# Query projection of the 32-head attentions by a seven-product block scheme, with single-buffered weights

## The reference, cut to what matters

```
q = rope(x @ Wq)      # 32 heads of 128: 512 -> 4096
k = rope(ctx @ Wk)    # 8 key heads of 128, each shared by 4 query heads
v = ctx @ Wv
p = softmax(q k^T / sqrt(128) + mask)      # per head and block, 128 x 128
x = layernorm(x + concat_heads(p v) @ Wo)  # 4096 -> 512
```

## Time and profile before

| | |
|---|---|
| median of 3 runs | 2799.91 us (2798.87 to 2800.82) |
| profiled execution, its own time | 2801.92 us |
| span of the profiled execution | 2800.6 us |
| mean granted TensorE clock | 0.987 of full speed |
| PE busy | 2658.8 us, 95% of the span |
| DVE, ACT, POOL busy | 59%, 30%, 16% |
| chain that ended last | PE 87%, DVE 7%, ACT 3% |

### The profile page before, as it was taken

How to read it: one execution, slowest core, us unless ns; L and a number is a source line. 1 busy time by engine, 2 the same in 40 slices (tenths; PEclk the granted TensorE clock), 3 DMA queues, 4 the chain that set the end, 5 groups by cost and what they waited for, 6 DMA issues and landing times.

```text
span 2800.6 us, 40463 instructions
## 1 busy us (share of the span) xinstructions
PE 2658.8 (95%) x15768; PEld 1764.9 (63%) x15768; DVE 1652.9 (59%) x3113; ACT 852.1 (30%) x2630; POOL 458.7 (16%) x511
## 2 busy tenths in 40 slices
PE   8999999999989899899999999899998898999998
PEld 7855666666665566556666666656774455576664
DVE  3557667776666456466676667664555644344455
ACT  0012222222233355222222222323444412333331
POOL 1022211222202100132122222022211121000002
PEclk9999999999999899999999999999999999999999
DMA  8631011100001100001111100010000010000000
GB/s 181 92 127 41 20 38 38 38 38 16 16 1 38 69 2 2 27 23 38 38 38 38 38 16 16 1 68 31 2 2 27 20 62 27 15 26 1 12 1 31
DMA packets 53821, 94.89 MB, mean 34 GB/s; under 512 B 29408, under 2 KB 38560, under 8 KB 47488
## 3 DMA queue, kind: packets, MB, share of 16 engines
q1 hardware_dynamic: 53632, 92.30, 10.8%
HBM read 83.89 MB, written 8.39 MB: 33 GB/s over the span
## 4 chain that ended last, share of the span: by engine, by line
PE 87%; DVE 7%; ACT 3%; issue 1%; DMA 1%; POOL 0%; DVEq 0%; SPq 0%; POOLq 0%; ACTq 0%
PE banks L628 19%; PE banks L666 13%; PE banks L620 4%; PE banks L687 4%; PE banks L1209 3%; PE banks L710 3%; PE banks L1719 3%; PE banks L303 3%; PE banks L1771 3%; PE banks L2009 2%; PE banks L2041 2%; PE banks L1748 2%; PE banks L2074 2%; PE banks L1724 2%; PE banks L650 2%; PE banks L697 2%
## 5 line engine op out<-in xcount | busy, mean ns | idle before, releaser
L628 PE MATMUL banks<-xT,weights 128*128 128x512 f32 x1024 | 458.2, 592 | 0.0
L748 ACT ACTIVATE E_x<-S_x,sm_x 128x128 f32<-128x128 f32 x512 | 199.3, 390 | 588.1 <-DVE sm_x L837 588.1
L628 PEld LDWEIGHTS banks<-xT,weights 128*128 128x128 f32 x1024 | 188.9, 190 | 209.5 <-issue 206.6
L887 POOL TENSOR_TENSOR QT<-QT,turned 128x512 f32<-128x512 f32 x128 | 162.4, 1269 | 708.2 <-DVE QT L781 506.5
L809 DVE TENSOR_TENSOR x<-banks,x 128x512 f32<-128x512 f32 x336 | 171.5, 510 | 143.7 <-PE banks L666 137.9
L779 DVE TENSOR_TENSOR turned<-banks,const 64x512 f32<-64x512 f32 x160 | 109.4, 684 | 233.1 <-PE banks L628 232.6
L666 PE MATMUL banks<-weights 128*128 128x256 f32 x896 | 223.8, 383 | 0.0
L161 POOL TENSOR_TENSOR norm_spread<-norm_mv,const 128x1 f32<-128x1 f32 x96 | 20.9, 218 | 1223.4 <-DVE norm_mv L157 1223.4
L666 PE MATMUL banks<-weights,OT 128*128 128x256 f32 x672 | 178.1, 387 | 25.1 <-DVE x L809 12.3
L666 PEld LDWEIGHTS banks<-weights 128*128 128x128 f32 x896 | 163.9, 191 | 44.4 <-DVE x L809 15.0
L666 PEld LDWEIGHTS banks<-weights,OT 128*128 128x128 f32 x672 | 120.5, 190 | 79.3 <-DVE x L809 38.8
(11 more groups left out here) (294 smaller groups left out, 4546.8 us busy)
## 6 DMA issues: line engine op xcount, KB each, us to landing
weights<-in_L_xwq SPq DMA_DIRECT2D x16, 1024.0 KB, 4.8
weights<-in_L_xwo SPq DMA_DIRECT2D x16, 1024.0 KB, 7.4
weights<-in_L_xwk SPq DMA_DIRECT2D x16, 256.0 KB, 5.1
weights<-in_L_xwv SPq DMA_DIRECT2D x16, 256.0 KB, 5.4
weights<-in_L_ffn_W_base SPq DMA_DIRECT2D x3, 1024.0 KB, 4.8
weights<-in_L_xwq SPq DMA_DIRECT2D x4, 768.0 KB, 5.0
weights<-in_L_xwo SPq DMA_DIRECT2D x4, 768.0 KB, 6.4
xT<-in_xT SPq DMA_DIRECT2D x4, 512.0 KB, 9.9
```

The costliest lines, as they stand in the source:

```text
L628: mm = PE.matmul(bank[:, :], weight, source[:, k, half_of(i)], start=k == 0, stop=k == KC - 1)
L748: ins = AC.activation(e[:, j, :], s[:, j, :], ACT.Exp, bias=sm[:, 0, j:j + 1], scale=1.0, accum_out=sm[:, 1, j:j + 1])
L887: PO.tensor_tensor(dst, dst, turned[j % 2][:, :, :], ALU.add).then_inc(*x_roped.one())
```

## The change

In the two stages, the query product of a group is done on 2x2 blocks as the output product is: the weights' blocks are two halves of the 512 inputs by two pairs of heads, x's blocks two halves of the inputs by two halves of the rows. For each p of 0 and 1, heads p and p+2 and both halves of the rows come out of seven products of two calls (128x512) each: 14 calls in place of 16. The four results are called C11, C12, C21, C22 (C12 and C22 are the second half of the rows).

The 8 query jobs become 6, three for each p: turn 0 is P2 and P1, turn 1 is P5, P6 and P3, turn 2 is P4 and P7. P1, P6 and P7 accumulate in bank 0, the others in bank 1. ACT copies what bank 1 holds into QT (after P2, P5, P3 and P4); DVE adds bank 0 to it, which makes a block of queries, and then makes the two sine products from QT in SBUF; POOL does the cosine product in place and the final add. A job waits for the DVE adds of the job just before it.

DVE makes sums of xT once a stage (`sums_of_xT`, eight operations of 128x512), POOL sums of each group's query weights (`wq_sums`, four). Wq, Wk and Wv have one buffer each: the next group's is loaded when the last product of the present one is done. The masked scores S go from three buffers to two. `ot_sums` and `wo_sums` change their form but keep four operations each. The last 16 units are plain in place of the last 8. `plans` becomes 2, 2, 1, 2, 1, 1, 1, 0 (first group: 1 in each step). Other stages only share semaphore names.

```diff
-                NJ, NR = 12, 10
-                order = (0, 1, 4, 5, 2, 3, 6, 7, 8, 9, 10, 11)
-                plans = [(1, 2, 2, 2, 1, 1, 1, 0)] + [(2, 2, 2, 2, 2, 1, 1, 0)] * (G8 - 2)
+                JOBS = (("k", 0), ("k", 1)) + tuple(("q", n) for n in range(6)) + (("v", 0), ("v", 1))
+                NJ, NR = len(JOBS), 10
+                opening = (("k", 0), ("k", 1), ("v", 0), ("v", 1)) + JOBS[2:8]
+                plans = [(1, 1, 1, 1, 1, 1, 1, 1)] + [(2, 2, 1, 2, 1, 1, 1, 0)] * (G8 - 2)
-                pairs = (units - B) // 2
+                pairs = (units - 2 * B) // 2
 # sp_cross
-                            SP.wait_ge(*x_proj(NR * (g + 1)))
-                            load_cross_qkv(layer, views, g + 2)
+                            SP.wait_ge(*x_keys(2 * g))
+                            SP.dma_start(views["wk"], dram[f"{layer}_xwk"][g]).then_inc(*xwk_in.one())
+                            SP.wait_ge(*x_query(4 * g))
+                            SP.dma_start(wq, dram[f"{layer}_xwq"][g]).then_inc(*xwq_in.one())
+                            SP.wait_ge(*xv_mm(2 * g))
+                            SP.dma_start(views["wv"], dram[f"{layer}_xwv"][g]).then_inc(*xwv_in.one())
 # pe_cross
+                        if n == 0:
+                            PE.wait_ge(xwq_in.sem, wq_base + 16 * (g + 1))
+                            PE.wait_ge(*x_taken(NR * g + 2))
...
+                        else:
+                            PE.wait_ge(*x_qadd(8 * g + 4 * p + (0, 1, 2)[turn]))
...
+                        if turn == 0:
+                            product("P2").then_inc(*x_other.one())
+                            product("P1").then_inc(*x_query.one())
+                        elif turn == 1:
+                            product("P5").then_inc(*x_other.one())
+                            product("P6")
+                            PE.wait_ge(*x_other_here(8 * g + 4 * p + 2))
+                            product("P3").then_inc(*x_other.one())
+                        else:
+                            product("P4").then_inc(*x_other.one())
+                            product("P7").then_inc(*x_query.one())
 # act_cross, at the place of the job in the step (after the exponentials for a first job)
+                            for n, name in (((1, "C11"),), ((2, "C22"), (3, "C12")), ((4, "C21"),))[turn]:
+                                AC.wait_ge(*x_other(8 * g + 4 * p + n))
+                                AC.activation(query(g, p, name), psum[1][:, :], ACT.Copy).then_inc(*x_other_here.one())
 # dve_cross
+                        blocks = (("C11",), ("C12",), ("C21", "C22"))[turn]
+                        first = 4 * p + turn
+                        for name in blocks:
+                            to = query(g, p, name)
+                            DV.wait_ge(*x_other_here(8 * g + 4 * p + {"C11": 1, "C12": 3, "C21": 4, "C22": 2}[name]))
+                            DV.tensor_tensor(to, psum[0][:, :], to, ALU.add).then_inc(*x_qadd.one())
+                        for m, name in enumerate(blocks, first):
+                            DV.wait_ge(*x_qadd(8 * g + m + 1))
+                            sines(NR * g + 2 + m, query(g, p, name)).then_inc(*x_taken.one())
 # pool_cross
+                    def rope(j, to, cosines):
+                        PO.wait_ge(*x_taken(j + 1))
+                        if cosines:
+                            PO.tensor_tensor(four(to), four(to), spread(cos128, 4), ALU.mult).then_inc(*pool_step.one())
+                            PO.wait_ge(*pool_step.all())
+                        PO.tensor_tensor(four(to), four(to), turned[j % 2][:, :, :], ALU.add).then_inc(*x_roped.one())
+                        for m in range(8):
+                            if m == 4 and 1 <= g and 8 * (g - 1) < 2 * pairs:
+                                wo_sums(g - 1)
+                            rope(NR * g + 2 + m, query(g, m // 4, ("C11", "C12", "C21", "C22")[m % 4]), True)
+                        if g + 1 < G8:
+                            wq_sums(g + 1)
```

More of the change, by code:

```diff
@@ L508, in load_cross @@
                 views["mask"] = a.load("mask")
+            views["xT_sums"] = [a.place(P, D) for _ in range(3)] + [place_rest(D) for _ in range(2)]
+            assert taken[0] <= rest.shape[1]
             return layer, views, a.here.all()
@@ L605, in pe_cross, with keys @@
                 def pe_cross():
-                    def job(g, i):
-                        bank = psum[i % 2]
+                    def keys(g, i):
                         if i == 0:
[L609 to L621, removed]
-                        else:
-                            source = ctxT if i < 2 else xT
-                            if g == 0 and i in (2, 3):
-                                PE.wait_ge(*before.here(4 * (i - 2) + 3))
@@ L631, in products, with job @@
+                    def job(g, kind, i):
+                        {"k": keys, "v": values, "q": queries}[kind](g, i)
                     def products(q, turn):
@@ L733, in act_cross @@
                     AC.wait_ge(*before.added)
-                    for i in range(NJ):
-                        if is_value(i):
-                            value_copy(0, i)
+                    for kind, i in opening:
+                        drain(0, kind, i)
                     for step in range(units + 3):
@@ L816, in add_plain @@
                             DV.tensor_tensor(x[:, b, :], psum[7][:, :], x[:, b, :], ALU.add).then_inc(*x_sum.one())
-                            norm.stats(b, x_sum(NA * pairs + b + 1))
+                            if u >= units - B:
+                                norm.stats(b, x_sum(NA * pairs + u - 2 * pairs + 1))
                     DV.wait_ge(*before.added)
@@ L821, in dve_cross @@
                         DV.wait_ge(*here)
-                    for i in range(NJ):
-                        if not is_value(i):
-                            rope(0, i)
+                    for kind, i in opening[:2]:
+                        drain(0, kind, i)
+                    sums_of_xT()
+                    for kind, i in opening[2:]:
+                        drain(0, kind, i)
                     for i in range(2):
-                        rope(1, i)
+                        drain(1, "k", i)
                     for step in range(units + 3):
```

258 lines of the change are left out of this document (165 added, 93 removed).

## The result

The kernel after takes **2922.0 us** (2918.2 to 2929.1, four runs) against 2800.0 for the kernel before on the same chip (2798.9 to 2800.8): ratio 1.044, interval 1.0425 to 1.0456. The forecast was 2947, range 2855 to 3005. The profiled execution is the longest of the four (2929.1, span 2927.8, against a span of 2800.6 before), so its own sum is 127 us.

What follows compares the result with a forecast made beforehand. PE was taken as the bound, with new waits outweighing its saving. A stage: opening 6.4, first group 14, full groups 5 x 8.1, group 6 8.8, group 7 -10.1, clock 14, sum 73.6; two 147, giving 2947 us, range 2855 to 3005.

Steps and rivals of the forecast that it cites:

- PE has no gaps: Full group: PE busy 84.3 of 85.1 us, so removing matmuls shortens the stage if nothing else enters the path; -48.4.
- The waits of steps 2 and 4: Full group: PE waits for `ot_sums` and the output add, 5.4 lost in step 2, 6.1 in step 4; net +8.1.
- The cause named for the waits: Steps 2 and 4: ACT's copy behind exponentials, adds and sines ahead of the output add, DVE standing for POOL's operations.
- The first group: Loop's first group: PE loses 21 waiting for helpers, less 3.44 saved and most of 2.8 lost before; +14.
- The clock of the full groups: Slow clock after long waits, 1.0 each, two waits a full group; about 14 waits a stage, +14.
- Opening: Jobs ahead of the loop: PE stands after each job, 9.7 in all, with 3.44 saved; about +6.4.
- Group 6: Saved products, five plain units for two pairs, step 2's wait and one before the first plain product; +8.8.
- group 7: Two pairs become three plain units and the old waits of its even steps go; -10.1.
- Faster: Rival: PE stays the bound, the output add in steps 2 and 4 ends in time; 2754, chance 0.07.
- Heavy: Rival: DVE and POOL stand in each other's way throughout; 3049, chance 0.10.
- Light: Rival: slower, with no waiting for POOL and no slow clock; 2859, chance 0.20.
- The load shows: Rival: single-buffered weight load holds q0 and q1 in step 1; 67 on top of the forecast, 3014, chance 0.02.

Runs made afterwards that it cites:

- e8: e6 with POOL's products with the query cosines left out (output not the reference's); 2780.0 us, ratio 0.9935.
- e10: e8 with three of four operations of POOL's Wq sums and of its Wo sums also left out from the second group on; 2770.7 us.
- e2: Kernel after with POOL's cosine product on the queries left out, its final add kept; 2922.2 us, ratio 1.044.
- e6: e5 with ACT's query copies and PT ahead of the exponentials and, in one-job steps, DVE's second output add ahead of that step's sines; 2852.4 us.
- e4: Kernel after with ACT's first copy of a step's first query job ahead of the four exponentials; 2904.2 us, ratio 1.038.
- e1: Kernel after with DVE's output add ahead of the sines in steps whose only job is a query job; 2886.2 us, ratio 1.031.
- e9: Kernel after with the load of the next group's Wq issued behind Wv's, some 24 us later; 2924.1 us, ratio 1.044.
- e11: e6 with the query cosine products moved from POOL to DVE, behind the sines, nothing left out; 2865.3 us, ratio 1.023.
- e5: e4 with DVE keeping the sines of a second job for the next step, behind its output add and scaling; 2908.1 us.
- e12: e11 with query rotations spread, one at each step's end, two in step 5, and POOL's Wo sums two blocks earlier; 2955.3 us, ratio 1.056.

## Why the prediction was right, and where it was off

**PE has no gaps, so its saving is real only if nothing takes its place.** Right on both counts: with POOL relieved and the order changed, e8's groups are 82.2, e10's 81.8; in the kernel after they are 92 to 95. The total came out 25 us below the forecast partly by luck, as errors cancelled: a stage's five full groups with their clock were forecast at +50.5 and measured at +41, the first group at +14 and measured at +21 to +22.

**The waits of steps 2 and 4.** Right in place, releaser and kind. Sizes: `ot_sums` 1.77 and 2.58 (forecast 1.8 and 2.6); the output add 2.70 and 2.71 (forecast 3.6 and 3.5). The second term was too large by 0.9: from the end of `ot_sums` to the end of the output add I counted 6.2 in step 2, and the trace shows 5.7 (438.3 to 444.0); and PE came to that wait 3.1 behind the end of `ot_sums`, where I counted 2.65. The waits of a full group are 8.7 to 10.5, 9.2 on average, in place of the 11.5 that were forecast.

**The cause named for the waits.** Its share fell. The forecast put 1.6 of step 2's 5.4 down to waiting for POOL; e2 takes the cosines away and gains nothing; its rows show another chain to the output add that is nearly as long (DVE's adds stand 0.56 for ACT's copy, and the fourth sine meets POOL again). Only when ACT's copies and the order on DVE are mended does POOL show (e6 to e8: 72 us). Neither alone is the cause. The Trainium skill, "SBUF — State Buffer", section Who interferes with whom, says that only the port pair shared by VectorE and GpSimd causes contention, by an exclusive lock. The trace agrees that these two hold each other up: the sine, with both inputs in SBUF, takes 0.69 alone and 1.66 beside a POOL operation, and POOL's 1.27 becomes 1.76.

**The first group.** +14 forecast, +21.2 and +21.8 measured. The waits were sized well: 21 forecast, 18.4 measured in the first stage and 20.5 in the second. e4 confirms the copy behind the exponentials as one main source; those for PT are as large (5.5). The mis-sized term is the clock there: with 4 for everything outside the full groups I had allowed for far less than the some 8 that this group alone lost.

**The clock of the full groups.** 2 a group forecast. 93.3 on average, less the 81.6 of PE at granted clock 1.00 (e1's full groups) and 9.2 of waits, leaves 2.5. About right on average, uneven from group to group. The rival that nothing but the slow clock is lost falls with it: e1's full groups, at granted clock 1.00, still last 88.9 against 85.0 before.

**Opening.** +6.4 forecast, +6.6 measured in both stages. The idle time of PE that the trace shows there, 8.2, is less than the 9.7 forecast; with the saved 3.44 the opening lost 10.0, so each of its seven waits cost some 0.26 more than its idle time. **Group 6** +8.8 against +7.5, **group 7** -10.1 against -12.0 and -10.5.

**The rivals.** "Faster" fell at the point that the forecast named: the output add is behind PE. "Heavy" fell: the groups are not 99. "Light" fell too, at 2859, but is nearer than "heavy". "The load shows" fell by e9: Wq's load is issued at 371.79 and is wanted behind 419, and 24 us of delay cost nothing. The Trainium skill, "Trainium Kernel Development and Optimization", section Best Practices, asks for double buffers to overlap loads with compute; that did not decide here. The two buffers of masked scores cost nothing either: DVE stood idle ahead of the mask (L939) 47 times, each time for PE's scores and never for the exponentials. One slip in the numbers: the middle between forecast and heavy case is 2998, and the range was given up to 3005.

**What stays open.** No complete kernel here beats the one before; the best is e6, 2852.4. e8 shows that 18 us below before is there if 11 us of POOL's work a group had another place. On DVE, busy 66.4 us of a group of e11, I found no order that takes it; whether one exists was not settled. About half of the first group's loss stayed open too (72.7 at best, with work left out in e10, where 66.15 - 3.44 is 62.7), and the opening's +6.6 was not tried.

## What to carry to other kernels

A product saved on the busiest engine is worth its time only if each step's helpers still end before it: list for each step what stands ahead of the result that the engine waits for, in program order on every helper, and not the helpers' busy shares (DVE 63 of 92 us here, and PE waits). When two chains to one result are about equally long, taking one away can leave the time as it was: an experiment with no effect clears a suspect only after the other chain has been shortened (e2 against e8). A wait moved is rarely a wait removed: after each edit read the waits again by releaser, as e1, e5 and e12 show.

## What was not expected of the hardware

That the same wait does not always lower the clock was read in the kernel before; in the kernel after it also happens between groups of one program. The output products behind a wait of 2.70 took 3.56 in one full group and 1.99 in another:

```profile
444.06 3.56 PE L720 MATMUL banks<-weights 128*128 128x256 f32 x8 [2.70 <-DVE x L910]
...
633.00 1.99 PE L720 MATMUL banks<-weights 128*128 128x256 f32 x8 [2.70 <-DVE x L910]
```

What was not expected is that a slow stretch can hide part of the next wait: in step 4 of the group of the second row the products ahead ran slow (3.54), and the output add was then waited for 1.13 instead of 2.71.

```profile
655.71 3.54 PE L720 MATMUL banks<-weights,OT 128*128 128x256 f32 x8 [2.59 <-DVE weights L893]
...
661.24 1.99 PE L720 MATMUL banks<-weights 128*128 128x256 f32 x8 [1.13 <-DVE x L910]
```
